# Cross attention on one core: one rstd for both halves of a batch, adds moved between GpSimd and VectorE, and a new order of the end

## The reference

```python
q = (x @ Wq.T + bq)   # [8, 224, 512] -> 16 heads
k = (ctx @ Wk.T + bk) # [8, 750, 512]
v = (ctx @ Wv.T + bv)
att = softmax(q k^T / sqrt(32))
out = x + (att @ v) @ Wo.T + bo
out = (out - mean) / sqrt(var + 1e-5) * gamma + beta   # per row of 512
```

## Time and profile before

| | us |
|---|---|
| median of 3 runs | 639.18 |
| profiled execution | 640.04 |
| its span | 637.3 |
| TensorE matmul busy | 611.6 (96%) |
| VectorE busy | 501.1 (79%) |
| GpSimd busy | 468.0 (73%) |
| ScalarE busy | 352.5 (55%) |
| one regular iteration | 74.0 |

### The profile page before, as it was taken

One profiled execution on the slowest core, in us unless ns is written; L12 is line 12 of the kernel. 1 busy time (PEld: TensorE's weight loads), 2 busy tenths in 40 slices (PEclk: granted clock), 3 DMA queues, 4 the chain that ended last, 5 costly groups with the idle time before them and its releaser, 6 DMA issues.

```text
span 637.3 us, 13655 instructions
## 1 busy us (share of the span) xinstructions
PE 611.6 (96%) x5217; PEld 425.4 (67%) x5217; DVE 501.1 (79%) x680; ACT 352.5 (55%) x673; POOL 468.0 (73%) x459
## 2 busy tenths in 40 slices
PE   8998999999999999999999999999999999899894
PEld 7766677766676676766677676766767666576542
DVE  4677787788797797887787887977878887757885
ACT  4514566556565465664665565664656656444661
POOL 9633677784987589784987759785897869775853
PEclk9999999999999999999999999999999999899998
DMA  9574532562245523754137532564237422421020
GB/s 304 186 183 126 133 78 72 133 145 70 65 110 142 129 63 89 151 127 125 38 86 167 143 77 62 115 147 118 69 88 169 96 62 51 107 69 25 2 59 29
DMA packets 95776, 67.02 MB, mean 105 GB/s; under 512 B 69780, under 2 KB 81760, under 8 KB 95712
## 3 DMA queue, kind: packets, MB, share of 16 engines
q1 hardware_dynamic: 95200, 65.41, 41.2%
q0 software_dynamic: 512, 0.75, 0.5%
HBM read 24.52 MB, written 3.67 MB: 44 GB/s over the span
## 4 chain that ended last, share of the span: by engine, by line
PE 69%; POOL 14%; DVE 12%; issue 3%; DMA 1%; ACT 1%; POOLq 0%; SPq 0%; DVEq 0%; ACTq 0%
PE ps_task L610 34%; PE ps_scores L626 10%; PE ps_scoresT L650 8%; PE ps_task L666 6%; POOL pair_sums L1036 6%; DVE top L928 4%; PE ps_task L564 4%; POOL head_sums L1041 3%; DVE token_parts L905 3%; POOL head_sums L1044 3%; PE ps_scores L610 2%; POOL rstd L1056 2%; PE ps_task L692 2%; DVE attn_sums L935 1%; DMA x_in<-in_x 1%
## 5 line engine op out<-in xcount | busy, mean ns | idle before, releaser
L809 ACT ACTIVATE probsT<-ps_scoresT 125x448 f32<-125x448 f32 x384 | 204.5, 544 | 154.2 <-PE ps_scoresT L650 148.4
L928 DVE TENSOR_REDUCE top<-ps_scores 112x1 f32<-112x750 f32 x256 | 234.2, 927 | 63.8 <-PE ps_scores L626 63.0
L1036 POOL TENSOR_TENSOR pair_sums<-probsT 125x672 f32<-125x672 f32 x122 | 197.8, 1621 | 72.3 <-ACT probsT L809 65.6
L650 PE MATMUL ps_scoresT<-stacks 100*125 100x224 f16 x768 | 135.8, 261 | 1.5 <-ACT probsT L809 1.2
L610 PE MATMUL ps_task<-wvT,ctxT 128*125 128x512 f16 x564 | 135.6, 379 | 0.1
L610 PE MATMUL ps_task<-ctxT,wkT 128*128 128x375 f16 x708 | 130.7, 323 | 0.0
L626 PE MATMUL ps_scores<-stacks 96*112 96x512 f16 (+1 forms) x512 | 125.6, 327 | 4.8 <-DVE top L928 4.0
L650 PEld LDWEIGHTS ps_scoresT<-stacks 100*125 100x125 f16 x768 | 94.5, 137 | 41.2 <-ACT probsT L809 4.9
L1041 POOL TENSOR_TENSOR head_sums<-pair_sums 125x224 f32<-125x224 f32 x122 | 96.6, 792 | 11.4
L610 PEld LDWEIGHTS ps_task<-wvT,ctxT 128*125 128x125 f16 x564 | 73.2, 136 | 33.1 <-DVE parts L885 0.4
L1044 POOL TENSOR_TENSOR head_sums<-head_sums,pair_sums 125x224 f32<-125x224 f32 x122 | 87.3, 715 | 9.6
(11 more groups left out here) (103 smaller groups left out, 533.7 us busy)
## 6 DMA issues: line engine op xcount, KB each, us to landing
stacks<-parts SPq DMA_DIRECT2D x248, 60.9 KB, 2.0
ctx_in<-in_ctx SPq DMA_DIRECT2D x8, 768.0 KB, 5.5
stacks<-parts SPq DMA_DIRECT2D x124, 46.9 KB, 2.0
resid<-in_x SPq DMA_DIRECT2D x8, 448.0 KB, 4.1
ctx_in<-in_ctx SPq DMA_DIRECT2D x7, 512.0 KB
out_y<-y SPq DMA_DIRECT2D x16, 224.0 KB, 2.3
x_in<-in_x SPq DMA_DIRECT2D x8, 256.0 KB, 3.1
stacks<-parts SPq DMA_DIRECT2D x124, 14.0 KB, 1.8
```

The costliest lines, as they stand in the source:

```text
L650: last = nc.tensor.matmul(ps_scoresT[0:KP, piece % 2, NQ * i:NQ * i + NQ], stacks[:, g, h, KP * k:KP * k + KP], stacks[:, g, h, Qc], start ...
L809: nc.scalar.activation(probsT[0:KP, g % 2, h, 2 * j:2 * j + 2, :].rearrange("p k q -> p (k q)"), ps_scoresT[0:KP, piece % 2, 0:2 * NQ], AC ...
L928: nc.vector.tensor_reduce(top[0:QP, g % 2, HG * q + h:HG * q + h + 1], ps_scores[0:QP, s % RING, 0:NK], AX.X, ALU.max).then_inc(top_ready, 1)
L1036: nc.gpsimd.tensor_tensor(pair_sums[0:KP], probsT[0:KP, g % 2, h, 0:3, :], probsT[0:KP, g % 2, h, 3:6, :], ALU.add).then_inc(pair_sums_rea ...
```

## The change

In iterations 1 to 7 GpSimd makes variance + eps and rstd for both halves at once, in step 23 and ahead of the third head's adds. Both gammas come in step 26. Beta of the first half stays with GpSimd (step 27), that of the second goes to VectorE (step 29). SyncE issues the second half of the next context's load ahead of the transposes of tiles 0 to 2, not between them.

For the end: attends of units 28 to 30 that are spread start one step earlier; unit 29's copy, inversions and scale stand all in step 0 of iteration 8 and its two parts in step 1. The gammas and betas of batch 6 are delayed to step 3 of iteration 8. VectorE's head sums of unit 30 are three adds each, with ctx_in as scratch, and the last one moves from step 0 to 1. GpSimd adds tiles 0, 1 and 2 of unit 31 for all four heads (two adds of 125x896), and TensorE's ones-matmuls take that sum and tiles 3 to 5, all behind the last attend. VectorE adds bo for the last batch. In iteration 8 GpSimd adds beta of the first half.

```diff
-    SPREAD = {**{("attend", k): (2, 2 + k) for k in range(KT)}, "sum_keys": (2, 7), ...
+    SPREAD = {**{("attend", k): (2, 1 + k) for k in range(KT)}, "sum_keys": (2, 7), ...
+    SUMMED_TILES = 3
-    TAIL = {NU - 3: {"copy": 0, ("invert", 0): 1, ("invert", 1): 2, "scale": 3, "high": 4, "low": 5},
+    TAIL = {NU - 3: {"copy": 0, ("invert", 0): 0, ("invert", 1): 0, "scale": 0, "high": 1, "low": 1},
...
-    GAMMA_STEPS = (3 * UNIT + 2, 3 * UNIT + 5)
+    RSTD_STEP = 3 * UNIT - 1
+    GAMMA_STEP, BETA_STEPS = 3 * UNIT + 2, (3 * UNIT + 3, 3 * UNIT + 5)
+    DELAYED_GAMMA_STEP = 3
...
@@ sync @@
                 if has_next(b):
-                    for i in range(2):
-                        turn_when_free(("ctxT", i))
                     wait_split(("ctxT", 2))
                     load_ctx(b + 1, 1)
-                    turn_when_free(("ctxT", 2))
+                    for i in range(3):
+                        turn_when_free(("ctxT", i))
...
+                if b == LAST:
+                    sp.wait_ge(task_saved, after(("O", 1)))
+                    load_resid(b)
                 if has_output(b):
                     for q in range(2):
                         store_half(q)
@@ tensor @@
+            def sum_last():
+                pe.wait_ge(first_tiles_added, SUMMED_TILES - 1)
+                for k in range(SUMMED_TILES - 1, KT):
+                    for h in range(HG):
+                        c = DK * h
+                        last = nc.tensor.matmul(ps_scores[c:c + DK, 0, BANK_COLS:BANK_COLS + NQ], ones[0:KP, :],
+                                                probsT[0:KP, g % 2, h, k, :] if k >= SUMMED_TILES else head_sums[0:KP, g % 2, h, :], ...
+                last.then_inc(sums_ready, 1)
@@ vector @@
+            def plus_beta(batch):
+                dve.wait_ge(y_scaled, 2 * batch + 2)
+                nc.vector.tensor_tensor(y[0:QP, 1], y[0:QP, 1], rows["beta"][0:QP], ALU.add).then_inc(second_ready, 1)
...
             def sum_head(u, g, h):
-                nc.vector.tensor_reduce(head_sums[0:KP, g % 2, h, :], probsT[0:KP, g % 2, h].rearrange("p k q -> p q k"),
-                                        AX.X, ALU.add).then_inc(last_sums_ready, 1)
+                nc.vector.tensor_tensor(pairs, probsT[0:KP, g % 2, h, 0:3, :], probsT[0:KP, g % 2, h, 3:6, :], ...
+                dve.wait_ge(pairs_added, n + 1)
+                nc.vector.tensor_tensor(head_sums[0:KP, g % 2, h, :], pairs[:, 0], pairs[:, 1], ALU.add).then_inc(two_added, 1)
+                dve.wait_ge(two_added, n + 1)
+                nc.vector.tensor_tensor(head_sums[0:KP, g % 2, h, :], head_sums[0:KP, g % 2, h, :], pairs[:, 2], ...
...
-                    if has_output(b) and s in GAMMA_STEPS:
+                    if has_output(b) and b != LAST and s == GAMMA_STEP:
                         dve.wait_ge(gamma_turned, 1)
-                        times_gamma(GAMMA_STEPS.index(s), b - 1)
-                        if isinstance(b, int) and b == B:
-                            last_beta(GAMMA_STEPS.index(s), b - 1)
+                        for q in range(2):
+                            times_gamma(q, b - 1)
+                    if has_output(b) and b != LAST and s == BETA_STEPS[1]:
+                        plus_beta(b - 1)
+                    if b == B and s == DELAYED_GAMMA_STEP:
+                        for q in range(2):
+                            times_gamma(q, LAST - 1)
+                        plus_beta(LAST - 1)
+                    if b == B and s == 9:
+                        add_bo(LAST)
@@ gpsimd @@
+            def add_first_tiles():
+                pool.wait_ge(sums_ready, u - 1)
+                for k in range(1, SUMMED_TILES):
+                    pool.wait_ge(probs_ready, PIECES * u + HG * (k // 2 + 1))
+                    ...
+                    nc.gpsimd.tensor_tensor(head_sums[0:KP, g % 2], probsT[0:KP, g % 2, :, 0, :] if k == 1 else head_sums[0:KP, g % 2],
+                                            probsT[0:KP, g % 2, :, k, :], ALU.add).then_inc(first_tiles_added, 1)
...
                 for s in range(STEPS):
+                    if has_output(b) and b != B and s == RSTD_STEP:
+                        rstd_of(slice(0, 2), b - 1)
                     for back, i, h in SUM_STEPS:
...
-                            if s == O_STEPS[q] + 2:
-                                rstd_of(q, b - 1)
+                            if b == B and s == O_STEPS[q] + 2:
+                                rstd_of(slice(q, q + 1), b - 1)
+                        if b != LAST and s == BETA_STEPS[0]:
+                            plus_beta(b - 1)
+                        if b == B and s == DELAYED_GAMMA_STEP:
+                            add_first_tiles()
+                            plus_beta(LAST - 1)
```

More of the change, by code:

```diff
@@ L256, in build @@
         rstd = sb("rstd", [P, 2])
[L257 to L258 removed]
+        eps = sb("eps", [P, 2])
+        minus_half = sb("minus_half", [P, 2])
         bias_rows = y[0:3 * DT, 0, 0:P]
@@ L916, in times_gamma, with add_bo @@
                                                ALU.mult, ALU.mult).then_inc(y_scaled, 1)
-            def last_beta(q, batch):
-                dve.wait_ge(y_scaled, 2 * batch + q + 1)
-                nc.vector.tensor_tensor(y[0:QP, q], y[0:QP, q], rows["beta"][0:QP], ALU.add).then_inc(last_ready, 1)
+            def plus_beta(batch):
+                dve.wait_ge(y_scaled, 2 * batch + 2)
+                nc.vector.tensor_tensor(y[0:QP, 1], y[0:QP, 1], rows["beta"][0:QP], ALU.add).then_inc(second_ready, 1)
+            def add_bo(batch):
+                dve.wait_ge(resid_loaded, DMA * (batch + 1))
+                for q in range(2):
+                    nc.vector.tensor_tensor(resid[0:QP, q], resid[0:QP, q], rows["bo"][0:QP], ALU.add).then_inc(resid_ready, 1)
             def row_max(s, T, unit):
@@ L987, in iteration @@
                         u = unit_before(b, g, back)
-                        if u is not None and s % UNIT == i and vector_sums(HG * u + h):
+                        if u is not None and s % UNIT == i + (back == 2) and vector_sums(HG * u + h):
                             sum_head(u, (g - back) % UNITS, h)
@@ L1050, in add_bo, with rstd_of, plus_beta @@
                 nc.gpsimd.tensor_tensor(resid[0:QP, q], resid[0:QP, q], rows["bo"][0:QP], ALU.add).then_inc(resid_ready, 1)
-            def rstd_of(q, batch):
-                pool.wait_ge(mean_ready, 2 * batch + q + 1)
-                nc.gpsimd.tensor_tensor(var_eps[0:QP, q:q + 1], mean_var[0:QP, q, 1:2], eps[0:QP], ALU.add).then_inc(var_eps_ready, 1)
-                pool.wait_ge(var_eps_ready, 2 * batch + q + 1)
-                nc.gpsimd.tensor_tensor(rstd[0:QP, q:q + 1], var_eps[0:QP, q:q + 1], minus_half[0:QP], ALU.pow).then_inc(rstd_ready, 1)
-            def plus_beta(q, batch):
-                pool.wait_ge(y_scaled, 2 * batch + q + 1)
-                nc.gpsimd.tensor_tensor(y[0:QP, q], y[0:QP, q], rows["beta"][0:QP], ALU.add).then_inc(y_ready, 1)
+            def rstd_of(halves, batch):
+                n = 2 * batch + halves.stop
+                pool.wait_ge(mean_ready, n)
+                nc.gpsimd.tensor_tensor(var_eps[0:QP, halves], mean_var[0:QP, halves, 1], eps[0:QP, halves],
+                                        ALU.add).then_inc(var_eps_ready, halves.stop - halves.start)
+                pool.wait_ge(var_eps_ready, n)
+                nc.gpsimd.tensor_tensor(rstd[0:QP, halves], var_eps[0:QP, halves], minus_half[0:QP, halves],
+                                        ALU.pow).then_inc(rstd_ready, halves.stop - halves.start)
+            def plus_beta(batch):
+                pool.wait_ge(y_scaled, 2 * batch + 1)
+                nc.gpsimd.tensor_tensor(y[0:QP, 0], y[0:QP, 0], rows["beta"][0:QP], ALU.add).then_inc(first_ready, 1)
             pool.wait_ge(task_saved, prologue.index(("Q", 1)) + 1)
```

46 lines of the change are left out of this document (27 added, 19 removed).

## The result

The changed kernel takes **640.80 us** (median of 20 runs, 638.53 to 642.36), the kernel before on the same chip 638.41 (20 runs, 637.12 to 640.56): ratio 1.0036, interval [1.0027, 1.0045]. It is slower by 2.4 us (difference of the medians); the forecast was 633.5 and faster.

The account below looks back on a forecast made before the run. TensorE was taken as the bound, with time to be had only where it waits, mainly the key sum. Terms -5.1 -1.2 -0.1 +0.45 = -5.95 us took 639.18 to 633.2, forecast as 633.5; range 8 in 10: 630.9 to 637.2.

Parts of the forecast that it names:

- Part 1: Iterations 1 to 6: one rstd before the third head's adds takes 0.55 us; head 3's sum comes 1.0 us earlier.
- Part 2: Step 26: second gamma delays GpSimd's last short add 0.1 us (0 to 0.4); with Part 1, -5.1 us in six iterations.
- rival C: Regular batches: rstd blocked again (1.56 us), third head only 0.1 to 0.4 us earlier; 636.9 us, chance 0.20.
- D: Rival: rstd blocked, mean not earlier, second gamma blocks last add; key-sum wait 1.1 to 1.5 us, 641.9 us; chance 0.09.
- the wait at 546: TensorE's 1.85 us wait for VectorE's stretched line 950: earlier GpSimd work gains 1.2 us, once; bounds 0 and 1.85.
- Part 3: Context's load issued ahead of three transposes: 0, bounds -0.1 and +0.1 us per batch.
- Part 4: Last batch: maxima turn 3.2 us earlier, spent again by VectorE's list before the projection; net -0.1, bounds -2.4 and +1.4 us.
- B: Rival: tail collisions small, projection starts at 620.9, released by TensorE's own sums; priced at 630.9 us, chance 0.14.
- Part 5: The end: GpSimd's beta of half 0 holds back the last gamma, +0.45 us; -0.45 if GpSimd did not block.

Follow-up runs that it names:

- run 1: Changed kernel with GpSimd's variance and rstd for both halves behind the third head's adds of step 23, not ahead of them: 631.95 us, ratio 0.9893.
- run 2: Changed kernel with the variance + eps operation left out (output without the 1e-5): 633.72 us, ratio 0.9927.
- run 10: Kernel of run 6 plus both gammas in step 26, second beta on VectorE in step 29 and the context's load first: 632.70 us, ratio 0.9906.
- run 5: Changed kernel with the last batch's two betas on VectorE, each right behind its gamma, as before: 640.1 us, ratio 1.0014.
- run 6: Kernel before with one edit: one variance and rstd for both halves, behind the third head's adds in step 23 (not last batch): 629.80 us, ratio 0.9864.
- run 9: Kernel of run 7 without GpSimd's tile adds in the last batch; TensorE sums all six tiles of unit 31 with ones: 628.95 us, ratio 0.9840.
- run 7: Kernel of run 1 with unit 29's high and low parts in step 3 of the last batch instead of step 1: 633.27 us, ratio 0.9908.
- run 3: Changed kernel with the second half's gamma back in step 29, ahead of its beta, in the regular batches: 637.52 us, ratio 0.9985.

## Why the prediction was wrong

**Part 1 is the step that failed:** "so rstd gets in first and takes 0.55". It took 1.77 us in six iterations. It is not the start of line 977 that blocks, but that it is next in VectorE's list while the row max runs; I had read this off and then measured my margin to the high part's arrival (380.16) instead of to the row max's start. The row max came 0.3 us earlier by the same quiet that brought the mean; rstd came 0.3 us later than I had it, half of it the mean and half the gaps. So it was 0.07 us behind. With rstd at 1.77 the third head starts about 0.15 us earlier instead of 1.0. Forecast -5.1 us; measured +1.05, and where the order is safe (run 1) -6.5: six times 74.03 - 72.94. The term was too large even for the port won: run 2 has -3.4. There the third head's add stretches line 977, where I had line 977 hold the add, and TensorE waits 0.4 us at line 613.

**Part 2's term was mis-sized:** second gamma's collision 0.1 us, measured 0.3, inside its bound of 0.4. The blocked rstd alone is rival C (third head 0.1 to 0.4 us earlier); with the second gamma on top the wait is 1.06, just short of D's 1.1 to 1.5. D's other conditions did not hold: the mean did come earlier, and the wait at 546 went. D had 0.09, and its argument against, "the quiet GpSimd around 378", was true and did not help.

**The wait at 546:** -1.2 forecast, -1.19 measured, by luck. The wait went whole, which brought the attend behind it 1.7 us forward; 0.36 us of that were lost again at the key sum of 551.33 and some 0.15 behind it. What the forecast did not see is iteration 7, where the moves of Part 2 cost 3 us (run 10).

**Part 3:** no engine waits for that load in the changed kernel's profile; it was not tried alone.

**Part 4:** the turn of the maxima came 2.7 us earlier (forecast 3.2). The projection was to stand 15.8 us behind it and stands 17.0. Two bounds lie close together. VectorE's list, the one named, gives 16.75 in run 5 where the clock stayed full. In the changed kernel's profile the lower clock behind the 1.78 us wait makes TensorE's own sums late instead: 618.40 - 611.48 = 6.9 us of it. There unit 30's low part is ready at 622.83, and the projection starts at 623.85 behind the sums, which was to be the sign of B and came from another cause. I had the wait (exponentials from 611.5) but not its price. Net measured +1.74, forecast -0.1 with +1.4 as the upper bound: outside it.

**Part 5:** right, +0.41 to +0.48 for +0.45.

**The baseline:** the first profile held a clock loss of 1.6 us behind the wait at 546 (598.08 against 596.34 at the same turn, less 0.13 from the start) that the second lacks. It made the changed kernel's profile look only 1.0 us longer; it changed no term of the sum. And by the forecast's own chances its range held 0.74, not 8 in 10: half of B, the rest of C and D lie outside.

Left open: why the clock falls behind a wait of 1.8 us in one execution and not in the next.

## What to carry to other kernels

Where two engines share a port and the one next in line claims it early, an order that depends on a margin of 0.2 us is no order. Put the small operation whose result is not urgent behind the long ones that something waits for, in the instruction list. Here that one edit is worth 8 us (run 6), and in the changed kernel the same operation a few lines earlier costs 9 (run 1). And before work is given to a second engine to shorten the first one's list, ask what the third one is doing then: two GpSimd adds that were to save TensorE 0.8 us cost 4.3 us net (run 9 against run 7).

## What the runs showed of the hardware

- GpSimd's rstd was held while a VectorE operation with two SBUF inputs was next in VectorE's list, even with a single-input reduce running: over 112x2 it took 1.77 us started 0.07 us behind the reduce (changed kernel), 0.70 started 0.26 us ahead of it (run 2), and 0.70 beside a reduce with a reciprocal next (597.02). Where between 0.26 ahead and 0.07 behind the order turns, no run shows. The held rstd ended 0.56 us after the VectorE operation's end. The Trainium skill (SBUF — State Buffer, SBUF: two separate sides) has it that whichever of such a VectorE operation and a GpSimd operation starts first gets the shared ports for the whole instruction. By the profile's start times the trace does not agree: rstd was there at 381.50, line 977 began at 382.27, and rstd lost. Whether VectorE had issued it by then no row shows.
- The other way, VectorE's short add (0.39) took 2.17 beside a GpSimd add over 896 columns, and two gammas 5.14 against 1.41.
- The rstd over two columns takes 0.70 where one column takes 0.55.
- Behind an idle time of TensorE of 1.78 us the granted clock was 0.51, the level of 1.2 GHz, for 6.9 us (611.50 to 618.40), with matmul groups at 0.98 against 0.59; behind 1.77 us in run 3 it fell only from 612.70 on, for 3.3 us, and behind 1.78 us in run 5 it was 1.00 until 620. Behind 1.85 us it was 0.50 from 548 to 550 in one execution and 1.00 in another.
